# The next image's attention front inside this image's state-space scan

## The chip, the cores and the metric

The kernel runs on one core of one Trainium2 chip. The metric is the device time of one launch in microseconds (us). The kernel before took 14195.23 us, the median of three runs (14193.28 to 14201.19). The engines are called PE (TensorE), DVE (VectorE), ACT (ScalarE), POOL (GpSimd) and SP (SyncE, which only issues DMAs here).

## What is computed

Sixteen images of 192 channels and 32 x 32 = 1024 tokens (L) pass one after the other through four blocks, each added to its input X after a group norm:

1. multi-head attention: 6 heads of 32, softmax over 1024 keys, output projection;
2. a selective scan in four directions (K = 4): per direction a low-rank projection gives dt, B and C; `dt = softplus(...)`, then for each channel d and state n the recurrence `h = h * exp(dt * A) + (dt * u) * B`, and `y = sum over n of h * C`; then layer norm, gelu;
3. a depthwise 3x3 convolution of which each channel keeps its 30 largest values;
4. a chunked state-space mixer with its own convolution, gate and output projection.

```
h = h * dA + (dtt * ut)[..., None] * bt[:, :, None, :]
y = jnp.einsum('bkdn,bkn->bkd', h, ct)
```

## The kernel before, in words

`build` loads the weights and then runs a hardware loop over the 16 images (`nc.Fori`, L1666). In one pass every engine has its own in-order program, and semaphores tie them together. The blocks follow one another: `norm_*` and `attn_*` (L366 to L660), `norm_*` and `scan_*` (L756 to L1048), `conv_*`, `mix_*`. At the end of a pass the semaphores are cleared and all engines meet in a barrier (L1738 to L1741). One image ends before the next begins; only the load of the next image into XI is issued early (L1672). A scratch area of SBUF, the arena, is given anew to each block.

Attention. The projections (L457) are fp32 matmuls on the normalised image XN. Scores are needed to nearly fp32, so q and k are split into three bf16 parts (copies on ACT L567 and L571, subtractions on DVE L611 and POOL L449, 18 small DMAs per head pair by `attn_sp` L440). For every head and block of 128 queries a rough score in bf16 (L480, `rough`) gives a row maximum (DVE `reduce_max` over 128 x 1024, L617); `max_rows` (L490) turns the maxima into a row that is folded into the scores (L532, bf16). ACT takes the exponential (L597) into PT, and L548 multiplies by the values, two heads side by side in 64 columns each. `invert` (L650) and `scale` (L657) divide by the sums; L559 projects out and L642 adds to X.

The front of the scan. XN and its transpose XT are multiplied by the low-rank weights (L774, L784), softplus is done on DVE, ACT, DVE (L937, L896, L899, L942), DU = dt * u on POOL and DVE (L1028, L947). dt, dt * u, B and C are stored to DRAM (L847 to L864) and read back spread over the partitions.

The scan itself has NSTEP = 96 steps. A partition holds one (channel, state) pair, 16 channels by 8 states at a time, and a step is one such tile of 128 x 1024:

- SP (`spread`, L838, L842) brings dt and dt * u of 16 channels, 512 KB each after spreading, once for two steps, into rings of RING = 3;
- ACT (L913) writes the decay exp(dt * A) into PSUM, in two buffers, ps[1] and ps[2] by turns;
- the input product dt * u * B goes into `step[i % NBUF]`, by POOL (L1036) in one step of three, else by DVE (L991); where DVE does an even step, B is read from a copy in PSUM, made by ACT (L908), in an odd step from SBUF;
- DVE (L995) runs the recurrence along the tokens, in place;
- POOL (L1048) multiplies by C, in place;
- for each batch of 4 steps PE (L799) sums the states into ps[3], 8 fp32 matmuls of 512 columns (16 instructions in the trace), and frees four of the NBUF = 9 buffers.

DVE's program for one step is: input product if it is its own (wait for PE's batch), wait for POOL's input, wait for the decay, recurrence. POOL's is: the input product of step i + LEAD, then wait for the recurrence i, then the product with C.

```
wait_input(dve, i)
dve.wait_ge(m_da, i + 1)
nc.vector.tensor_tensor_scan(step[i % NBUF][:, o], ps[1 + i % 2][:, o], step[i % NBUF][:, o], 0.0, ALU.mult, ALU.add).then_inc(m_h, 1)
```

## Time and profile before

| | |
|---|---|
| median of three runs | 14195.23 us |
| the profiled execution | 14205.94 us |
| its span | 14204.1 us |
| busy share PE, DVE, ACT, POOL | 61%, 67%, 30%, 44% |
| mean granted TensorE clock | 0.708 of 2.4 GHz |
| image 0 begins | 39.88 us |
| image 3: attention and front of the scan | 2698 to 2982 us |
| image 3: 96 scan steps | 2982 to 3330 us |
| image 3: end of the scan, convolution, mixer | 3330 to 3584 us |

An engine's idle time costs only where nothing else sets the end; the three stages follow each other, so each is read alone. In the clock column 1.00 is 2.4 GHz and 0.50 is 1.2 GHz.

### The profile page before, as it was taken

The page shows a single profiled execution, that of the slowest core. Times are in us where ns is not written, and L with a number is a line of the kernel's source. Part 1 is how long each engine was busy: PE and PEld are TensorE (multiplying, and loading weights), DVE is VectorE, ACT ScalarE, POOL GpSimd, SP SyncE. Part 2 cuts the span into 40 slices and gives each one's busy share as a digit, 9 for nine tenths or more (in the row PEclk, how much of TensorE's full clock was granted, in tenths as well). Part 3 has the DMA queues.
Part 4 walks back from the last instruction along what each step waited for, and adds up shares of the span by engine and source line. Part 5 has one row for each costly group of instructions (what it writes and reads, how often), then busy time and mean ns, then how long its engine had stood idle before and what let it go on. Part 6 is the DMA issues. An engine that isn't in the chain of part 4 may idle for free. (4 is left out here: it accounts for less than half of the span.)

```text
span 14204.1 us, 88128 instructions
## 1 busy us (share of the span) xinstructions
PE 8617.6 (61%) x26672; PEld 2789.1 (20%) x26816; DVE 9455.2 (67%) x8214; ACT 4329.4 (30%) x4371; POOL 6226.0 (44%) x2937
## 2 busy tenths in 40 slices
PE   6475664746647466484664846648466484664846
PEld 2031221212212122121221312213122131221312
DVE  4856748567485674856758577585775857758576
ACT  2323233232332323323233232322323223232232
POOL 1815518155171551715417154271642716427164
PEclk8676776767767677676776767767676676776767
DMA  2505225052250512505135051340513405134061
GB/s 74 138 16 134 55 70 134 16 138 50 75 129 16 142 46 78 126 16 144 44 83 121 16 148 40 85 119 16 151 37 85 119 16 151 37 89 115 16 155 35
DMA packets 364229, 1164.38 MB, mean 82 GB/s; under 512 B 61487, under 2 KB 63039, under 8 KB 363599
## 3 DMA queue, kind: packets, MB, share of 16 engines
q1 hardware_dynamic: 358363, 1155.62, 32.3%
q8 instruction: 238, 3.90, 0.1%
q14 instruction: 392, 3.21, 0.1%
q10 hardware_dynamic: 3988, 1.01, 0.0%
q0 software_dynamic: 1248, 0.64, 0.0%
HBM read 959.86 MB, written 121.63 MB: 76 GB/s over the span
## 5 line engine op out<-in xcount | busy, mean ns | idle before, releaser
L799 PE MATMUL ps<-arena,sel_y 128*32 128x512 f32 x6144 | 2216.9, 888 | 3817.3 <-POOL arena L1048 3817.3
L1048 POOL TENSOR_TENSOR arena<-arena 128x1024 f32<-128x1024 f32 x1536 | 3721.7, 2449 | 29.4 <-DVE arena L995 29.4
L995 DVE TENSOR_TENSOR_SCAN arena<-ps,arena 128x1024 f32<-128x1024 f32 x1536 | 3475.8, 2284 | 66.9 <-POOL arena L1036 22.6
L913 ACT ACTIVATE ps<-arena,v_na 128x1024 f32<-128x1024 f32 x1536 | 1712.4, 1117 | 3797.8 <-DVE arena L995 3110.6
L1036 POOL TENSOR_TENSOR arena<-arena 128x1024 f32<-128x1024 f32 x512 | 1235.4, 2413 | 822.6 <-DMA arena<-scan_dtu 717.5
L799 PEld LDWEIGHTS ps<-arena,sel_y 128*32 128x32 f32 x6144 | 474.5, 151 | 5570.4 <-POOL arena L1048 3509.2
L617 DVE TENSOR_REDUCE arena<-ps 128x1 bf16<-128x1024 f32 x768 | 933.8, 1223 | 922.9 <-PE ps L480 922.4
L1028 POOL TENSOR_TENSOR arena<-arena,XN 128x1024 f32<-128x1024 f32 x32 | 75.2, 2350 | 2839.5 <-DVE arena L942 2839.5
L991 DVE TENSOR_TENSOR arena<-arena,ps 128x1024 f32<-128x1024 f32 x768 | 919.3, 1197 | 565.5 <-DMA arena<-scan_dtu 355.5
L597 ACT ACTIVATE arena<-ps 128x1024 f32<-128x1024 f32 x768 | 744.5, 1021 | 970.6 <-PE ps L532 970.6
L548 PE MATMUL ps<-arena 128*64 128x512 f32 x3072 | 773.0, 627 | 3.5 <-DVE arena L611 3.5
L532 PE MATMUL ps<-arena 65*128 65x512 bf16 (+1 forms) x2928 | 727.7, 384 | 64.1 <-ACT arena L597 29.2
L480 PE MATMUL ps<-arena 32*128 32x512 bf16 x1536 | 578.7, 468 | 105.8 <-DVE arena L617 84.8
L361 PE MATMUL ps<-g_mv,c_group 128*128 128x3 f32 (+1 forms) x512 | 136.9, 363 | 814.4 <-DVE g_mv L332 814.4
L650 DVE RECIPROCAL arena<-arena 128x256 f32<-128x256 f32 (+1 forms) x128 | 326.2, 2548 | 409.1 <-ACT arena L605 407.6
L991 DVE TENSOR_TENSOR arena<-arena 128x1024 f32<-128x1024 f32 x256 | 577.2, 2255 | 0.0
L449 POOL TENSOR_TENSOR arena<-arena 128x1024 bf16<-128x1024 f32 x48 | 101.1, 2120 | 999.5 <-ACT arena L571 999.5
L1235 PE MATMUL ps<-XN,w_x 64*128 64x512 f32 (+3 forms) x512 | 508.2, 1126 | 36.5 <-DVE XN L353 36.5
L1491 POOL TENSOR_SCALAR arena<-arena,v_mcw 128x640 f32<-128x640 f32 x144 | 164.3, 1144 | 701.3 <-ACT arena L1389 701.3
L937 DVE TENSOR_SCALAR arena<-ps,v_dtb 128x1024 f32<-128x1024 f32 x96 | 123.2, 1283 | 520.7 <-PE ps L784 520.7
L1481 DVE SCALAR_TENSOR_TENSOR arena<-arena,v_mcw 128x1024 f32<-128x1024 f32 (+1 forms) x384 | 456.9, 1190 | 13.1
L1636 POOL MEMSET arena<- 128x4624 f32 x16 | 63.2, 3951 | 909.2 <-DVE X L1121 909.2
(213 smaller groups left out, 11961.2 us busy)
## 6 DMA issues: line engine op xcount, KB each, us to landing
arena<-scan_dt SPq DMA_DIRECT2D x768, 512.0 KB, 4.7
arena<-scan_dtu SPq DMA_DIRECT2D x768, 512.0 KB, 6.0
arena<-scan_bc SPq DMA_DIRECT2D x256, 512.0 KB, 6.2
arena<-arena SPq DMA_DIRECT2D x1152, 64.0 KB, 2.0
scan_dt<-arena SPq DMA_DIRECT2D x64, 512.0 KB, 10.9
scan_dtu<-arena SPq DMA_DIRECT2D x64, 512.0 KB, 8.9
scan_dt<-arena SPq DMA_DIRECT2D x64, 256.0 KB, 12.4
scan_dtu<-arena SPq DMA_DIRECT2D x64, 256.0 KB, 12.5
```

Of the source, the lines that this page charges most:

```text
L480: mm = nc.tensor.matmul(P[:, HALF * m:HALF * m + HALF], q[:, Q * j:Q * j + Q], k[:, HALF * m:HALF * m + HALF], start=True, stop=True)
L532: mm = nc.tensor.matmul(P, k[0:n, 2 * t + e, Q * j:Q * j + Q], q[0:n, 2 * t + e, HALF * m:HALF * m + HALF], start=(n == MAIN), stop=(n == ...
L548: mm = nc.tensor.matmul(ps[2][64 * e:64 * e + 64, HALF * m:HALF * m + HALF], V[:, j - 1, 2 * t + e, :], PT[:, 2 * ((j - 1) % 2) + e, HALF ...
L597: nc.scalar.activation(PT[:, 2 * (j % 2) + e, :], ps[e][:], ACT.Exp, scale=DH ** -0.5).then_inc(a_e, 1)
L617: nc.vector.reduce_max(MX[:, i:i + 1], P[:], AX.X).then_inc(a_m, 1)
L799: mm = nc.tensor.matmul(ps[3][32 * q:32 * q + 32, HALF * h:HALF * h + HALF], sel_y[:, r, :], step[i % NBUF][:, HALF * h:HALF * h + HALF], ...
L913: nc.scalar.activation(ps[1 + i % 2][:], dtr[:, i // 2 % RING, :], ACT.Exp, scale=v_na[:, at:at + 1]).then_inc(m_da, 1)
L991: nc.vector.tensor_tensor(step[i % NBUF], dur[:, i // 2 % RING, :], states, ALU.mult).then_inc(m_buv, 1)
L995: nc.vector.tensor_tensor_scan(step[i % NBUF][:, o], ps[1 + i % 2][:, o], step[i % NBUF][:, o], 0.0, ALU.mult, ALU.add).then_inc(m_h, 1)
L1036: pool.tensor_tensor(step[i % NBUF], dur[:, i // 2 % RING, :], Bb[:, 2 * (k // 2) + f, :], ALU.mult).then_inc(m_bup, 1)
L1048: pool.tensor_tensor(step[i % NBUF], step[i % NBUF], Cb[:, 2 * (k // 2) + f, :], ALU.mult).then_inc(m_hc, 1)
L1235: mm = nc.tensor.matmul(ps[p][0:n, half(h)], w[0:m, c, lo:lo + n], XN[0:m, c, half(h)], start=(c == 0), stop=(c == 1))
```

## The change

The work is cut in two. The **front** of an image is its group norm, attention, second norm and everything up to dt, dt * u, B and C in DRAM. The rest is the 96 steps and what follows. Before the loop the front of image 0 runs alone; in the loop, pass b does the rest of image b with the front of image b + 1 woven into its 96 steps. (The front of a seventeenth image, a copy of the first, is done in the last pass.)

The weave is written out by hand. `front_pe`, `front_act`, `front_dve`, `front_pool` and `front_sp` are Python generators over HS = 192 half steps `hs`, two for each step, and each `scan_*` calls `next(front)` twice in a step:

```diff
+            for i in range(NSTEP):
+                next(front)
+                wait_input(dve, i)
+                dve.wait_ge(m_da, i + 1)
+                ...tensor_tensor_scan(step[:, i % NBUF, o], ps[2][:, o], step[:, i % NBUF, o], 0.0, ...)
+                next(front)
...
+                if i + 1 < NSTEP and not on_pool(i + 1):
+                    state_input(i + 1)
```

The plan: norm at hs 4 to 9; `project` hs 10 to 21; `values` hs 22 to 25; rough scores and their maxima from hs 16, 52 and 88, one a half step; units of scores, exponentials and head sums from hs 52 and 88 every second half step and from hs 124 every half step; output projection hs 142 and 147; second norm hs 148 to 154; low-rank projections hs 155 to 159; dt from hs 161 to 183.

```diff
+        ROUGH = [16, 52, 88]
+        UNITS = [(52, 2), (88, 2), (124, 1)]
+        DT_AT = (161, 163, 165, 172, 174, 176)
+        LN_AT = (169, 180)
+        DT_END = (170, 171, 172, 181, 182, 183)
```

The space is cut so that both fit. PSUM: ps[3] stays with the sums, ps[2] is the only decay buffer (ACT writes the decay of step i + 1 after the recurrence of step i), ps[0] and ps[1] are four half banks of 512 columns for the front. SBUF: rings of DTR = 2 and DUR = 3, NBUF = 8 step buffers, LEAD = 2. B is read from SBUF alone; its copy in PSUM goes away.

```diff
         def on_pool(i):
-            return i % 2 == 1 and i // 2 % 3 != 2
+            return i % 4 != 1
```

```diff
+            def decay(i):
+                act.wait_ge(m_dtl[i // 2 % DTR], 16 * (i // 2 // DTR + 1))
+                if i:
+                    act.wait_ge(m_h, i)
+                nc.scalar.activation(ps[2][:], dtr[:, i // 2 % DTR, :], ACT.Exp, ...).then_inc(m_da, 1)
```

Attention is rewritten for half banks. The three-way bf16 split with its copies and 54 small DMAs is gone: scores are single fp32 matmuls over 33 rows (32 of the head and one that carries the maximum), two heads at partitions 0 and 64, and the rough scores read the high halves of the same fp32 words as bf16. There are 96 rough tiles of 128 x 512 where there were 48 of 128 x 1024, and 48 units of 512 queries where there were 24 of 1024.

```diff
+                else:
+                    pe.wait_ge(a_m, 32 * t + r)
+                nc.tensor.matmul(bank(3), QR[at:at + DH, t, Q * j:Q * j + Q],
+                                 KR[at:at + DH, t, HALF * m:HALF * m + HALF], start=True, stop=True).then_inc(a_s, 1)
...
+                for e in range(2):
+                    r = slice(64 * e, 64 * e + DH + 1)
+                    nc.tensor.matmul(bank(e), KK[r, t, Q * j:Q * j + Q], QQ[r, t, HALF * m:HALF * m + HALF],
+                                     start=True, stop=True).then_inc(a_st, 1)
```

`project` pads each head to 64 columns, so it makes 12 half tiles (24 fp32 matmuls) where there were 6 (12). All six DU products are POOL's. PE's sums of batch n come in step 4n + 5, between the two half steps:

```diff
+            for i in range(NSTEP):
+                next(front)
+                if i % BATCH == 1 and i > BATCH:
+                    sums(i // BATCH - 1)
+                next(front)
```

At the start of a pass SP loads B, C, dt and dt * u of the first steps from DRAM, and the image after attention (X, YA) too, which the front of the pass before has stored (`x1_d`, `xn_d`). POOL's `conv_pool` also waits for the front's last stores (`f_out`). The convolution and the mixer are unchanged.

## Rows read from the trace of the kernel before

**Rows 1.** Page, section 1: busy us (share of the span), instructions

```profile
PE 8617.6 (61%) x26672; PEld 2789.1 (20%) x26816; DVE 9455.2 (67%) x8214; ACT 4329.4 (30%) x4371; POOL 6226.0 (44%) x2937
```

**Rows 2.** Windows, three stages: us, PE, PEld, DVE, ACT, POOL busy, clock, DMA share, GB/s

```profile
2698.00:2982.00 284.00, 214.09 (x647) 67.61 (x656) 124.18 (x123) 95.25 (x94) 19.96 (x8) 0.73 0.20 55
2982.00:3330.00 348.00, 133.60 (x368) 28.49 (x368) 309.58 (x163) 112.14 (x102) 307.56 (x128) 0.67 0.65 163
3330.00:3584.00 254.00, 189.80 (x652) 78.11 (x652) 157.65 (x227) 63.07 (x78) 60.24 (x46) 0.73 0.00 1
```

**Rows 3.** Lines by form, 2982 to 3330: busy us, mean ns, idle before, releaser

```profile
L1048 POOL TENSOR_TENSOR arena<-arena 128x1024 f32<-128x1024 f32 x96 | 232.6, 2449 | 1.9 <-DVE arena L995 1.9
L995 DVE TENSOR_TENSOR_SCAN arena<-ps,arena 128x1024 f32<-128x1024 f32 x96 | 217.2, 2284 | 3.9 <-POOL arena L1036 1.1
L913 ACT ACTIVATE ps<-arena,v_na 128x1024 f32<-128x1024 f32 x95 | 106.0, 1117 | 227.7 <-DVE arena L995 194.9 <-DMA arena<-scan_dt 32.8
L1036 POOL TENSOR_TENSOR arena<-arena 128x1024 f32<-128x1024 f32 x32 | 77.1, 2409 | 51.5 <-DMA arena<-scan_dtu 43.6 <-PE ps L799 7.8
L991 DVE TENSOR_TENSOR arena<-arena,ps 128x1024 f32<-128x1024 f32 x48 | 57.5, 1197 | 34.6 <-DMA arena<-scan_dtu 21.0 <-issue 13.6
L991 DVE TENSOR_TENSOR arena<-arena 128x1024 f32<-128x1024 f32 x16 | 36.3, 2268 | 0.0
```

**Rows 4.** Timeline, POOL and DVE in the steps: start us, us, engine, line, count

```profile
3059.22 3.35 POOL L1048 TENSOR_TENSOR arena<-arena 128x1024 f32<-128x1024 f32 x1
...
3063.82 4.47 DVE L995 TENSOR_TENSOR_SCAN arena<-ps,arena 128x1024 f32<-128x1024 f32 x2
...
3091.23 9.26 POOL L1048 TENSOR_TENSOR arena<-arena 128x1024 f32<-128x1024 f32 x4
```

**Rows 5.** Timeline, PE's sums of two whole batches (16 instructions each)

```profile
3069.53 5.65 PE L799 MATMUL ps<-arena,sel_y 128*32 128x512 f32 x16 [7.41 <-POOL arena L1048]
...
3330.11 5.09 PE L799 MATMUL ps<-arena,sel_y 128*32 128x512 f32 x16 [5.65 <-POOL arena L1048]
```

**Rows 6.** Timeline, one turn of rough score and maximum in attention

```profile
2837.26 1.94 PE L548 MATMUL ps<-arena 128*64 128x512 f32 x8
2837.37 1.23 DVE L617 TENSOR_REDUCE arena<-ps 128x1 bf16<-128x1024 f32 x1 [1.16 <-PE ps L480]
...
2839.13 0.60 PE L480 MATMUL ps<-arena 32*128 32x512 bf16 x2
...
2839.77 1.23 DVE L617 TENSOR_REDUCE arena<-ps 128x1 bf16<-128x1024 f32 x1 [1.17 <-PE ps L480]
```

**Rows 7.** Windows of attention, PE alone: us, PE busy, clock, DMA share, GB/s

```profile
2720.00:2765.00 45.00, 42.29 (x76) 0.50 0.29 71
2770.00:2825.00 55.00, 50.25 (x212) 1.00 0.12 29
```

**Rows 8.** Timeline, PE's fp32 projections, and PE in attention after a gap

```profile
2715.67 16.07 PE L457 MATMUL ps<-XN,w_qk 128*128 128x512 f32 x16 [2.38 <-DVE XN L353]
...
2830.43 3.68 PE L548 MATMUL ps<-arena 128*64 128x512 f32 x8
...
2931.07 14.02 PE L784 MATMUL ps<-arena,w_dt 12*128 12x512 f32 x16
```

**Rows 9.** Lines by form, 2698 to 2982: operations that the front keeps

```profile
L650 DVE RECIPROCAL arena<-arena 128x256 f32<-128x256 f32 x4 | 7.0, 1744 | 0.0
...
L896 ACT ACT_TABLE_LOAD x2 | 2.6, 1283 | 0.0
```

**Rows 10.** Timeline, the turn from image 2 to 3, and the start of image 0

```profile
39.88 5.21 POOL L444 MEMSET arena<- 1x6144 bf16 x1 [17.73 <-POOLq L1658]
...
2697.79 0.68 DVE L1591 TENSOR_TENSOR X<-X,ps 64x512 f32<-64x512 f32 x1 [0.32 <-PE ps L1318]
...
2708.13 2.47 DVE L320 BATCH_NORM_STATS2 g_st<-XI 128x6 f32<-128x512 f32 x4 [9.66 <-issue]
```

**Rows 11.** DMA at the start of the steps: a window (PE busy, clock, share, GB/s)

```profile
2980.00:2985.00 5.00, 0.00 (x0) 0.50 1.02 236
```

More of the change, by code:

```diff
@@ new lines, in build, with bank, unit_at, rough_at @@
+        DT_END = (170, 171, 172, 181, 182, 183)
+        def bank(i):
+            return ps[i // 2][:, HALF * (i % 2):HALF * (i % 2) + HALF]
+        def unit_at(hs):
+            for t, (at, pitch) in enumerate(UNITS):
+                if 0 <= hs - at < 16 * pitch and (hs - at) % pitch == 0:
+                    return t, (hs - at) // pitch
+            return None, 0
+        def rough_at(hs):
+            for t, at in enumerate(ROUGH):
+                if 0 <= hs - at < 36:
+                    return t, hs - at
+            return None, 0
@@ L912, in scan_act @@
+        def scan_act(act, front):
+            def decay(i):
+                _, k, j, _, _, f = STEPS[i]
+                act.wait_ge(m_dtl[i // 2 % DTR], 16 * (i // 2 // DTR + 1))
+                if i:
+                    act.wait_ge(m_h, i)
                 at = 24 * k + 2 * j + f
-                nc.scalar.activation(ps[1 + i % 2][:], dtr[:, i // 2 % RING, :], ACT.Exp,
+                nc.scalar.activation(ps[2][:], dtr[:, i // 2 % DTR, :], ACT.Exp,
                                      scale=v_na[:, at:at + 1]).then_inc(m_da, 1)
+            decay(0)
+            for i in range(NSTEP):
+                next(front)
+                if i + 1 < NSTEP:
+                    decay(i + 1)
+                next(front)
@@ L1745, in _ @@
             def _(sp):
-                sp.wait_ge(s_x, 48 * (n_batch + 1))
+                sp.sem_inc(s_out, 1)
+                for _ in front_sp(sp, 0):
+                    pass
+                front_stored(sp)
+            @block.tensor
+            def _(pe):
+                for _ in front_pe(pe):
+                    pass
+            @block.scalar
+            def _(act):
+                for _ in front_act(act):
+                    pass
+            @block.vector
+            def _(dve):
+                for _ in front_dve(dve):
+                    pass
@@ new lines, in _ @@
+            @block.gpsimd
+            def _(pool):
+                for _ in front_pool(pool):
+                    pass
+        clear()
+        with nc.Fori(0, n_batch) as b:
+            with nc.Block() as block:
+                @block.sync
+                def _(sp):
+                    scan_sp(sp, b, front_sp(sp, b + 1))
+                    front_stored(sp)
+                    sp.wait_ge(b_x, 4)
+                    for c, m in enumerate(CT):
+                        sp.dma_start(out[b, 128 * c:128 * c + m, :], X[0:m, c, :]).then_inc(s_out, 16)
+                @block.tensor
+                def _(pe):
+                    scan_pe(pe, front_pe(pe))
+                    norm_pe(pe, 2)
+                    conv_pe(pe)
+                    norm_pe(pe, 3)
+                    mix_pe(pe)
+                @block.scalar
+                def _(act):
+                    scan_act(act, front_act(act))
+                    norm_act(act, 2)
+                    conv_act(act)
+                    norm_act(act, 3)
+                    mix_act(act)
+                @block.vector
+                def _(dve):
+                    scan_dve(dve, front_dve(dve))
+                    dve.wait_ge(m_x, 4)
+                    norm_dve(dve, 2, lambda t, n: XPv[0:n, t, 1:1 + H, 1:1 + W], begun=True, room=k_z)
+                    conv_dve(dve)
+                    dve.wait_ge(k_x, 2)
+                    norm_dve(dve, 3, lambda t, n: XN[0:n, t, :])
+                    mix_dve(dve)
+                @block.gpsimd
+                def _(pool):
+                    scan_pool(pool, front_pool(pool))
+                    conv_pool(pool)
+                    mix_pool(pool)
+            clear()
@@ L1747, in _ @@
+        with nc.Block() as block:
+            @block.sync
+            def _(sp):
                 sp.wait_ge(s_out, 32 * n_batch + 1)
```

995 lines of the change are left out of this document (488 added, 507 removed).

## Prediction

> **What bounds the kernel now.** I read the shares first, and they say little: DVE is busy 67% of the span, ACT and POOL less [rows 1]. The windows say why. One image is three stages in series: 284 us of attention and front of the scan, in which PE is busy 214 and POOL 20; 348 us of scan steps, in which DVE is busy 310 and POOL 308 but PE 134; and 254 us of the rest [rows 2]. Together 886, and (14204 - 40) / 16 = 885 from the start of image 0 [rows 10]. In the first stage PE and chains through it set the pace, in the second DVE and POOL share it at 348 / 96 = 3.6 us a step, with two thirds of PE and ACT unused. The grouped lines of the steps show what fills them: recurrence 2.28, product by C 2.45, decay 1.12, input products 1.20 to 2.41 us, and 50 us in which POOL's inputs waited, mostly for a DMA [rows 3].
>
> **What goes.** The serial 284 us are taken out of each image. 9.7 of them remain, the barrier between two images [rows 10]. The front runs 17 times, once by itself. So the question is how long 96 steps take with a front in them; at 3.6 us a step they would save 4000 us, and they can't.
>
> **POOL.** It has 96 products by C, 72 input products (32 before) and 6 DU: 174 operations. Back to back one is 9.26 / 4 = 2.31 us; one that meets a DVE operation with two SBUF inputs is 3.35 [rows 4], as DVE's own is 2.27 with both inputs in SBUF where 1.20 do with one in PSUM [rows 3]. 24 input products on DVE and 6 maxima of softplus are of that kind now: 174 x 2.31 + 30 x 1.0 = 432 us, 4.3 to 4.5 a step. That is the floor, 84 over before. Moving inputs from DVE to POOL costs this; it makes room on DVE.
>
> **DVE in the rough stage.** 96 maxima of 128 x 512: a two-operand operation of that width is 0.68 [rows 10], so 0.62 in a row. Each needs a new rough score, since one half bank serves both: from the end of a maximum at 2838.60 to PE's start at 2839.13 is 0.53, and PE ends 0.04 before the next [rows 6]; with one matmul for two, 0.38, the turn is 0.95. A step has two maxima, one turn hidden under the recurrence (4.47 for two, so 2.2 [rows 4]), one not: 2.2 + 2 x 0.62 + 0.95 = 4.4. Every fourth step an input product of 2.3 fills that turn, 1.35 more. The single decay buffer (0.1 + 1.12 after the recurrence) is hidden by it. Where nothing stands there it makes 3.6 a step, under POOL's 4.3, so I cost it at nothing.
>
> **PE's sums.** A batch is 5.1 to 5.7 us when it begins at 1.2 GHz, 3.4 (16 x 0.215, from 8 in 1.94 less the last one's tail) at 2.4 [rows 5, 6]. It stands between the two half steps, ahead of a rough score for which DVE waits: it starts some 1.9 us into a step of which 4.4 are DVE's, so DVE is late by about 2.7, or 1.0 at full clock, every fourth step.
>
> **Steps, in order.** Each term is per image.
> - Steps 0 to 4, POOL's pace with the norm: 5 x 4.5 = 22.
> - Steps 5 to 12, two `project` or `values` a step. 16 instructions took 16.07 [rows 8]: 4.0 for a half tile at 1.2 GHz, near 2.0 at 2.4. With rough scores and sums a step is 10.2 or 5.4. The sums of step 5 raise the clock just before, so I take nearer the low end, 6.75: 54.
> - Steps 13 to 25, rough scores alone, PE mostly idle and so slow: 4.4 + (1.35 + 2.7) / 4 = 5.4; the last two are light: 70.
> - Steps 26 to 61, rough scores with a unit every step. Scores: 4 instructions over 33 rows, 0.85 each at 1.2 GHz by the 12-row ones [rows 8], so 3.4, half of it at full clock, and half again if two row groups run side by side; no row shows two of those. Two column groups do: L548, 8 in 1.94, is twice as fast as one after the other [rows 6]. I take side by side, 0.86 or 1.7; head sums the same. At 2.4 GHz all this fits beside DVE: 4.4 + (1.35 + 1.3) / 4 = 5.1. At 1.2 the rough score behind them comes 1.1 late and the sums 3.8: 6.9; one after the other, 8.6. Reciprocals (1.74 for 256 columns [rows 9]) and scales (0.68 like the one in [rows 10]) add 0.3. I take 5.7: 205.
> - Steps 62 to 69, two units a step. ACT's two exponentials of 0.6 and the hand-overs make 2.2 a unit, 3.5 at 1.2 GHz, plus the decay: 5.6 to 8; 6.1: 49.
> - Steps 70 to 95: 26 x 1.75 x 2.31 = 105 for POOL's products, 14 for DU, 12 for contention, 8 for two turns of ACT through table loads (1.28 [rows 9]) and three logarithms (each like a decay's 1.12), which hold up the decay behind them, 3 for slow projections before waiting copies: 142.
> - Start of a pass: barrier 9.7, then the first B, dt and dt * u from DRAM and POOL's first input, 14 more: 24. Queued there are some 17 loads of 512 KB at 240 GB/s [rows 11], 2.2 us each, so dt of step 4 lands about 12 late; two reloads of B and C later, 5: 17.
>
> Sum: 24 + 17 + 22 + 54 + 70 + 205 + 49 + 142 = 583, where 9.7 + 274 + 348 stood; with 254, **837 an image** for 885.
>
> Alone, the first front has nothing to hide in: 63 for projections at 1.2 GHz, 50 for the first rough scores, 2 x 68 with units, 45 for the last units, 66 for norm and dt, 360 in all. Setup 40 and 6 for its new loads of weights. 46 + 360 + 16 x 837 = 13800. The profiled execution was 14206 and the median 14195, which I treat as one.
>
> Nothing for: the copy of B into PSUM (7 us of ACT, hidden now), the 54 small DMAs, `f_out` (the last store is 3 steps old by then), PE's extra projection columns beyond the above. If the stores of the front come late, POOL's clearing of the border waits, and 254 grows by that.
>
> **The clock, row against rule.** PE was busy 42.3 of 45 us with projections and rough scores and the granted clock was 0.50, 1.2 GHz, throughout; then with bf16 scores over 128 rows and head sums it was 1.00 [rows 7]. Later, after a pause of PE, 8 instructions of head sums took 3.68 us where 1.94 is usual [rows 6, 8]. By the Trainium skill, "TensorE: Matmul & The Clock Gate", Part 1, sustained activity releases the throttle. By that rule every dense stretch here would run at 2.4 GHz and the sum is that of the second rival. The trace disagrees for the first 45 us, so I keep both ends. And "TensorEngine Tiling (Array Packing)", Key Properties, says that a change of tiling mode drains the array. The new PE program changes it several times a step, and no row here prices that.
>
> **Rivals.**
> 1. *Slower: PE stays at 1.2 GHz while units and rough scores share it*, and the weave turns from DVE's pace to PE's. It speaks for it that 33-row and 32-row matmuls, like L480 and L784, ran slow for tens of us [rows 7, 8]; against, that sums and head sums lift the clock [rows 5, 8]. Steps 26 to 61 at 7.2 are 259, 5 to 12 at 8.5 are 68, 62 to 69 at 7.5 are 60: 837 + 54 + 14 + 11 = 916, so 15060. It decides at 862 an image, that is at 6.4 us a step in 26 to 61.
> 2. *PE at 2.4 GHz wherever it is dense*: 5 to 12 at 5.4, 26 to 61 at 5.1, 62 to 69 at 5.6, sums of 1.0: 837 - 11 - 22 - 4 - 6 = 794, with a first front of 310: 13060.
> 3. *POOL is the bound throughout*, the front hides wholly: 24 + 17 + 432 + 254 = 727: 12040. Against it is the 4.4 + 1.0 chain, which no overlap shortens.
> 4. *It doesn't overlap*, since in-order engines wait for one another and each half step costs a whole chain. Then 274 and 348 add up as before, with 17 more for loads: 893 with the 254, 14690.
>
> **How the numbers follow.** My forecast 0.43, rival 1 0.24, rival 2 0.16, rival 3 0.08, rival 4 0.09. A measurement tells 0.2%, 28 us, from nothing. Nearly all of the forecast's spread (13400 to 14250) is faster: 0.41 + 0.16 + 0.08 = 0.65; same 0.04; slower 0.31. Range 12850 to 15050: it leaves out rival 3 and the upper half of rival 1.
>
> **What would show it.** Right: no serial attention; steps of 5 to 6 us in the rough half and about 4.4 in the last quarter, POOL over 85% busy there, DVE idle before maxima with PE as releaser, clock over 0.75 in steps 26 to 61. Wrong: steps over 6.4 there with PE over 90% busy at 1.2 GHz, PE instructions of the two heads not overlapping, DVE waiting for the decay, or long waits for DMA at a pass's start.

## The result, and the profile after

The changed kernel takes 14225.58 us, median of 20 runs (14209.24 to 14267.94), against 14199.47 us for the kernel before on the same chip: a ratio of 1.0021 [1.0014, 1.0028], the brackets being the 95% interval. The overlap works and brings nothing. The profiled execution's span is 14223.4 us, 19.3 more than before.

The page's shares show what moved. PE and POOL have more to do than in [rows 1], DVE a little less:

```profile
PE 9387.0 (66%) x27880; PEld 2830.3 (20%) x27880; DVE 9347.3 (66%) x8534; ACT 4515.9 (32%) x5590; POOL 7951.4 (56%) x3576
```

The balance comes from one instruction, the first of the mixer on POOL: count, shortest/median/longest in ns, first and last start in us (in the kernel before the same clearing, L1636, starts first at 746.4 and last at 14014.1).

```profile
L1741 POOL MEMSET arena<- x16: 3951/3951/3951, 1171.0 to 14032.4; 128x4624 f32 x16
```

A pass lasts (14032.4 - 1171.0) / 15 = 857.4 us where an image took 884.5. That gains 15 x 27.1 = 406 us. But the first mixer starts 424.6 us later, since the first image's front has nothing to hide in. 424.6 - 406.4 + 1.0 at the end is 19. So two amounts of equal size stand against each other, and each had to be forecast well.

One whole pass in windows (window, us, then busy us of PE, PEld, DVE, ACT, POOL, granted clock, DMA share, GB/s). The cuts are: last X of the pass before, recurrences of steps 0, 5, 13, 26, 62 and 70, last sums, last X. They answer to [rows 2].

```profile
3925.90:3948.80 22.90, 0.00 (x0) 0.00 (x0) 0.00 (x0) 2.40 (x2) 3.31 (x2) 0.57 0.65 166
3948.80:3995.10 46.30, 6.82 (x14) 3.19 (x16) 22.54 (x23) 8.45 (x8) 21.24 (x10) 0.50 0.71 170
3995.10:4040.10 45.00, 42.83 (x118) 14.07 (x114) 30.26 (x20) 17.74 (x24) 35.74 (x16) 0.96 0.46 111
4040.10:4104.30 64.20, 31.77 (x92) 7.46 (x94) 46.54 (x40) 15.71 (x15) 52.58 (x22) 0.61 0.43 107
4104.30:4328.50 224.20, 175.94 (x503) 39.64 (x501) 163.62 (x127) 81.15 (x113) 156.30 (x65) 0.68 0.44 105
4328.50:4376.00 47.50, 41.88 (x164) 10.11 (x160) 36.38 (x17) 25.83 (x42) 34.91 (x15) 1.00 0.31 78
4376.00:4528.60 152.60, 74.81 (x166) 19.51 (x168) 119.98 (x69) 61.10 (x60) 129.62 (x51) 0.67 0.46 131
4528.60:4783.00 254.40, 189.49 (x652) 77.37 (x652) 156.94 (x227) 63.08 (x78) 60.19 (x45) 0.73 0.00 0
```

The serial 284 us are gone and the steps take 580 to the last sums instead of 348. The stretch to understand is the fifth row, steps 26 to 61: 36 steps at 6.2 us, in which no engine is full (PE 78%, DVE 73%, POOL 70%). The grouped lines of that stretch tell what ends DVE's idle time (busy us, mean ns, then idle us before and its releasers):

```profile
L1097 DVE TENSOR_TENSOR_SCAN arena<-ps,arena 128x1024 f32<-128x1024 f32 x36 | 81.7, 2269 | 1.3 <-ACT ps L1037 1.3
L820 DVE TENSOR_REDUCE arena<-ps 128x1 bf16<-128x512 f32 x64 | 43.9, 685 | 57.8 <-PE ps L609 57.7
L833 DVE RECIPROCAL arena<-arena 128x256 f32<-128x256 f32 x8 | 13.9, 1741 | 2.4 <-ACT arena L755 2.4
L1073 DVE TENSOR_TENSOR arena<-arena 128x1024 f32<-128x1024 f32 x9 | 12.8, 1419 | 0.1
L838 DVE TENSOR_TENSOR arena<-arena 32x512 f32<-32x512 f32 x6 | 12.7, 2124 | 0.2
```

These are the recurrence (L1097), the maxima (L820), the reciprocals (L833), the input products (L1073) and the scales (L838), which divide the head sums by their denominators. 163.6 busy and 57.7 waiting for a rough score make 221 of the 224 us. DVE is either at work or waits for PE's next rough score, and hardly anything else: 4.54 + 1.60 us a step. The variants below are read by this split.

What PE did just ahead of each rough score sorts the 57.7 us (worked out from the trace's instructions): 32.9 stand behind a batch of sums (8 times, 4.1 each), 17.4 behind scores and head sums (32 times, 0.54 each), 7.4 behind another rough score (24 times).

How such a wait comes about, in the timeline (start, us, engine, line; in brackets the idle time before):

```profile
4252.47 4.08 PE L939 MATMUL ps<-arena,sel_y 128*32 128x512 f32 x16
...
4256.48 0.40 PE L609 MATMUL ps<-arena 32*128 32x512 bf16 x1
...
4256.91 0.69 DVE L820 TENSOR_REDUCE arena<-ps 128x1 bf16<-128x512 f32 x1 [3.64 <-PE ps L609]
4257.52 2.28 DVE L1097 TENSOR_TENSOR_SCAN arena<-ps,arena 128x1024 f32<-128x1024 f32 x1
```

A batch of sums takes PE 4.08 us. Behind it stands a rough score of 0.40. For this DVE waits 3.64 us, and behind DVE's maximum stands the recurrence. This is the chain that the forecast had, in its place; it is only longer.

### The profile page after: what moved, and what is told of

Read it like the earlier page. It is cut to its first block and busy times, and to the rows that moved or that the text cites. A ratio compares the mean times of both kernels' runs of the same rounds, so it can differ in the third digit from the quotient of the medians.

```text
span 14223.4 us, 93061 instructions
## 1 busy us (share of the span) xinstructions
PE 9387.0 (66%) x27880; PEld 2830.3 (20%) x27880; DVE 9347.3 (66%) x8534; ACT 4515.9 (32%) x5590; POOL 7951.4 (56%) x3576
## 5 line engine op out<-in xcount | busy, mean ns | idle before, releaser
L1150 POOL TENSOR_TENSOR arena<-arena 128x1024 f32<-128x1024 f32 x1536 | 3865.2, 2517 | 1964.4 <-DVE arena L1097 1953.4
L1097 DVE TENSOR_TENSOR_SCAN arena<-ps,arena 128x1024 f32<-128x1024 f32 x1536 | 3495.7, 2276 | 770.6 <-ACT ps L1037 688.7
L1137 POOL TENSOR_TENSOR arena<-arena 128x1024 f32<-128x1024 f32 x1152 | 2846.9, 2471 | 1369.1 <-DMA arena<-scan_dtu 1018.4
L939 PE MATMUL ps<-arena,sel_y 128*32 128x512 f32 x6144 | 1994.2, 805 | 844.4 <-POOL arena L1150 844.4
L820 DVE TENSOR_REDUCE arena<-ps 128x1 bf16<-128x512 f32 x1632 | 1116.7, 684 | 1547.2 <-PE ps L609 1546.0
L609 PE MATMUL ps<-arena 32*128 32x512 bf16 x1632 | 823.8, 505 | 1033.5 <-DVE arena L820 1033.4
L763 ACT ACTIVATE arena<-ps 128x512 f32<-128x512 f32 x1632 | 885.0, 594 | 1805.2 <-PE ps L637 1805.2
L637 PE MATMUL ps<-arena 33*128 33x512 f32 x3264 | 1208.3, 825 | 155.4 <-ACT arena L763 80.2
L649 PE MATMUL ps<-arena 128*64 128x512 f32 x3264 | 1179.5, 809 | 27.9 <-ACT arena L763 20.1
L1073 DVE TENSOR_TENSOR arena<-arena 128x1024 f32<-128x1024 f32 x384 | 707.2, 1842 | 2.0
L833 DVE RECIPROCAL arena<-arena 128x256 f32<-128x256 f32 x204 | 355.0, 1742 | 226.0 <-ACT arena L755 226.0
L1568 POOL TENSOR_TENSOR arena<-arena,c_heads 88x1536 bf16<-88x1536 bf16 x112 | 313.2, 2797 | 204.2 <-ACT arena L1522 196.2
L637 PEld LDWEIGHTS ps<-arena 33*128 33x128 f32 x3264 | 306.1, 229 | 584.6 <-ACT arena L763 285.7
```

The source lines that it names most:

```text
L609: nc.tensor.matmul(bank(3), QR[at:at + DH, t, Q * j:Q * j + Q], KR[at:at + DH, t, HALF * m:HALF * m + HALF], start=True, stop=True).then_i ...
L637: nc.tensor.matmul(bank(e), KK[r, t, Q * j:Q * j + Q], QQ[r, t, HALF * m:HALF * m + HALF], start=True, stop=True).then_inc(a_st, 1)
L649: mm = nc.tensor.matmul(bank(2)[64 * e:64 * e + 64, :], V[:, j, 2 * t + e, :], PT[:, 2 * (u % 2) + e, :], start=(j == 0), stop=(j == 7))
L763: nc.scalar.activation(PT[:, 2 * (u % 2) + e, :], bank(e), ACT.Exp, scale=DH ** -0.5).then_inc(a_e, 1)
L820: nc.vector.reduce_max(MXH[:, i // 2, i % 2:i % 2 + 1], bank(3), AX.X).then_inc(a_m, 1)
L939: mm = nc.tensor.matmul(ps[3][32 * q:32 * q + 32, HALF * h:HALF * h + HALF], sel_y[:, r, :], step[:, i % NBUF, HALF * h:HALF * h + HALF], ...
```

## The experiments

14 kernels were run, each an edit of the changed kernel where nothing else is said. "A pass" is the distance between the first recurrences of two passes in the trace, the mean unless a range is given; it is 857.4 us for the changed kernel. "A pass less" or "more" is against that. The ratios are to the kernel before. The diffs show the lines that matter; `...` marks what is left out.

**1. The front ahead of the steps instead of among them** (all five engines alike):

```diff
-                    scan_dve(dve, front_dve(dve))
+                    for _ in front_dve(dve):
+                        pass
+                    scan_dve(dve, iter(range(HS)))
```

> In each pass the front of the next image runs to its end before the first scan step; nothing else is changed. The first front alone took about 463 us in the changed kernel (60 to 503), the steps alone are bound by GpSimd at 4.3 us a step by my count, 410, with some 50 for barrier and loads and 254 for the rest. If the weave hides the shorter part as planned: 463 + 410 + 50 + 254 = 1177 a pass, 19300 in all, and the weave is worth 300 us a pass. Rival: the weave hides little, and the new front is cheap when it is alone: under 950 a pass, 15700.

Measured: 19011.18 us, ratio 1.3395 [1.3372, 1.3417], a pass of 1155 (1151 to 1158). The overlap itself is real: it is worth 298 us a pass against the same operations in series. Its steps alone take 410 us from the first to the last recurrence, in the middle 4.3 a step with POOL busy all the time, as this window of 36 such steps shows:

```profile
3380.00:3535.60 155.60, 49.71 (x144) 10.69 (x144) 100.84 (x48) 40.73 (x37) 155.60 (x65) 0.68 0.62 151
```

So the forecast's floor for POOL (4.3 to 4.5) was right. But from the last X of a pass to the next first recurrence it is 485 us; less 23 for barrier and loads, 462 are left for the front by itself, where the kernel before has 274 and the forecast took 360. And in its middle PE stays at half clock, 85% busy:

```profile
2960.00:3080.00 120.00, 101.46 (x216) 20.56 (x216) 37.32 (x49) 24.54 (x46) 0.00 (x0) 0.50 0.00 0
```

**2. Load of the next image's start later**, behind the first dt, so that the first decay comes sooner:

```diff
             spread_dt(0)
+            next(front)
             outputs(0)
...
-                next(front)
+                if i:
+                    next(front)
```

> The load of the next image's X is issued after the first dt and dt*u instead of behind some 13 loads of a pass's start. In the changed kernel VectorE waits 20 us for it in step 2, with recurrence 2 queued behind. Theory (a load behind others stops an in-order engine): step 2 starts 15 to 20 us earlier, of which the later loads of dt and C take 3 to 6 back: 11 to 16 us a pass, 180 to 260 in all, 13970 to 14050. Rival (the loads themselves are the bound at the start of a pass): the wait moves to dt and dt*u, under 4 us a pass, 14160 or more.

Measured: 14112.3 us, ratio 0.9942 [0.9925, 0.9958], 7 us a pass less. Between the two theories: the norm's wait for the image (20 us) goes, and DVE waits 12 us for ACT's part of the norm instead, which stands on ACT behind a decay whose dt is 14 us late, and 5 for decays.

**3. A batch's sums in two halves**, the first between the half steps, the second after the second:

```diff
...
-                    sums(i // BATCH - 1)
+                    sums(i // BATCH - 1, (0,))
                 next(front)
+                if i % BATCH == 1 and i > BATCH:
+                    sums(i // BATCH - 1, (1,))
```

> TensorE's sums of four steps are cut into their two half banks, one between the half steps and one after. Theory (VectorE waits for the rough score queued behind the sums, some 2.7 us every fourth step in steps 5 to 61): about 1.5 of it goes, 14 batches, 20 us a pass, 320 in all, 13900. Rival (TensorE is full in these steps, at 1.2 GHz, and its work is only moved): within 5 us a pass, 14150 to 14300; splitting may also keep the clock down, which would make it slower.

Measured: 13811.43 us, ratio 0.9735 [0.9718, 0.9751], 26 us a pass less: steps 13 to 25 took 57 instead of 64, 26 to 61 208 to 210 instead of 224. The hold of 4 us in front of a rough score is on the path. The granted clock in steps 26 to 61 rose as well, from 0.68 to 0.74, but that isn't what gained: DVE's waiting behind sums fell from 32.9 to 16.4 us, and behind scores and head sums it didn't fall (17.4 and 19.8).

**4. Scores in bf16**, to take work from PE without changing the order; leaves out the low halves of q and k:

```diff
-                    nc.tensor.matmul(bank(e), KK[r, t, Q * j:Q * j + Q], QQ[r, t, HALF * m:HALF * m + HALF],
+                    nc.tensor.matmul(bank(e), KR[r, t, Q * j:Q * j + Q], QR[r, t, HALF * m:HALF * m + HALF],
```

> The scores are made from the bf16 high halves alone, one instruction a head for two; the low halves of q and k are left out. Theory (TensorE at 1.2 GHz binds steps 26 to 61): it saves 0.43 to 0.86 us a unit, 48 units, and the rough score behind it comes earlier by as much: 20 to 35 us a pass, 350 to 550 in all. Rival (VectorE's own chain of maximum, turn, maximum and recurrence binds): under 8 us a pass, over 14100.

Measured: 14035.14 us, ratio 0.9887 [0.9871, 0.9904]. 27 us less of PE in steps 26 to 61 (149.0 for 175.9) bring 7; the first front, where PE is busy most of the time, got 80 us shorter (first recurrence at 442.2 instead of 522.4). That the steps gain so little has a second reason besides VectorE's chain. The waiting for rough scores fell by 18 us (57.7 to 39.6), but DVE's own work rose by 10.6 (163.6 to 174.2), because its nine input products took 2.84 us each instead of 1.42:

```profile
L1073 DVE TENSOR_TENSOR arena<-arena 128x1024 f32<-128x1024 f32 x9 | 25.6, 2844 | 0.1
```

They now meet more of POOL's products; what is won in one wait comes back in part as contention. The granted clock fell to 0.64, too. So this run doesn't show by itself that PE's work is nearly free in the steps.

**5. Sums in quarters**, with the later load of experiment 2:

```diff
-                if i % BATCH == 1 and i > BATCH:
-                    sums(i // BATCH - 1)
+                if i % BATCH < 2 and i >= BATCH:
+                    sums(i // BATCH - 1, (2 * (i % BATCH),))
                 next(front)
+                if i % BATCH < 2 and i >= BATCH:
+                    sums(i // BATCH - 1, (2 * (i % BATCH) + 1,))
...
```

> Based on the two changes measured before it (load of the next image later: 7 us a pass less; sums of a batch in two halves: 24 a pass less), with each batch's 16 matmuls now in quarters of four, one at the end of each half step from step 4n+4 to 4n+5. Theory (what costs is the longest stretch for which PE keeps a rough score waiting, so that halving it again gives about half as much again): 24 x 0.4 = 10 us a pass more, 13811 - 113 - 160 = about 13540. Rival (the first quarter now stands half a step after the product it needs, PE waits there for POOL with a rough score behind it, or the halves already hid under the recurrence): no further gain, 13700 or more.

Measured: 14044.89 us, ratio 0.9889 [0.9872, 0.9905], on the rival's side, and far above its 13700. The sums took PE 2996.6 us in the run instead of 2065.7 with halves and the later load (experiment 9). A quarter held two matmuls into the same 32 output columns, where a half holds both output tiles side by side.

**6. The rough score ahead of scores and head sums** in each half step:

```diff
+                if t is not None and 0 < r < 32:
+                    rough(t, r)
                 t, k = unit_at(hs)
                 if t is not None:
                     scores(t, k)
...
-                if t is not None and r < 32:
+                if t is not None and r == 0:
                     rough(t, r)
```

> In each half step PE's rough score goes ahead of the scores and the head sums instead of behind them. Theory (DVE's 57.7 us of idle time before maxima in 225 us of steps 26 to 61 come from rough scores that stand behind 2.2 to 4 us of scores and head sums): some 0.8 us a step less over 36 steps and a little in the two groups before, 30 us a pass, about 13750. Rival (PE itself is what is full in these steps, or the scores now wait for the maximum and with them the exponentials, so only the order changes): within 5 us a pass, 14150 to 14300.

Measured: 14388.38 us, ratio 1.014 [1.0123, 1.0157]: both theories missed, 11 us slower in steps 26 to 61. DVE's waiting for rough scores rose from 57.7 to 68.2 us. ACT's for scores went from 86.2 to 135.9. That fits a rough score which waits for its maximum and now keeps the scores behind it waiting, as the rival said.

**7. The scales left out** (the division by the denominators; the twelve 32 x 512 products become a clearing of the same cells):

```diff
-                            nc.vector.tensor_tensor(OA[...], OC[r:r + 32, :], RD[r + 32:r + 64, :], ALU.mult)
+                            nc.vector.memset(OA[...], 0.5)
```

> Leaves out the division of the head sums by their denominators: the twelve products of 32 x 512 of a front, 2.04 us each beside GpSimd and 0.68 without, are replaced by clearing the same cells. Theory (small VectorE operations with two SBUF inputs wait for a whole GpSimd operation, and this waiting is on the path): 12 x 1.8 = 20 us a pass less, 13900 to 13950. Rival (VectorE waits for PE right after them in any case, so their waiting is taken out of a later wait): 5 us a pass or less, 14150 or more.

Measured: 14059.42 us, ratio 0.9904 [0.9887, 0.992], 10.4 us a pass over the whole run, between the two. In steps 26 to 61 DVE's busy time fell by 6.8 us and the steps by 3.8: a good half of what DVE is spared counts, the rest becomes waiting for PE (57.7 to 60.2).

**8. The overlap alone, with the input products split as before** (64 by VectorE, 32 by GpSimd):

```diff
-            return i % 4 != 1
+            return i % 2 == 1 and i // 2 % 3 != 2
...
+            state_input(0)
```

> The overlap alone: VectorE makes 64 of the 96 input products and GpSimd 32, as before the change. Theory (VectorE's chain of maximum, recurrence, maximum, input product sets the step, and GpSimd has room): 40 more products on VectorE, each 1.84 to 2.3 us of which one turn of the rough score is filled, some 1.1 net each: 44 us a pass slower, about 14900. Rival (GpSimd is the bound, it drops from 174 operations to 134): up to 40 us a pass faster in the steps, 13600. If both share it, near 14225.

Measured: 14504.11 us, ratio 1.0221 [1.0204, 1.0238], 17 us a pass more. A window of steps 26 to 61:

```profile
4188.20:4420.80 232.60, 173.31 (x504) 39.38 (x503) 209.20 (x143) 81.31 (x113) 123.08 (x49) 0.69 0.39 100
```

DVE has 46 us more to do than in the changed kernel and the steps take 8 more; the rest fills waits for PE (57.7 to 19.4).

**9. The two edits that gained, together** (experiments 2 and 3).

> Both edits that gained alone, together: the sums of a batch in two halves (24 us a pass less) and the load of the next image's start behind the first dt (7 us a pass less). If they act in different steps, as their traces say (the one in steps 13 to 61, the other in steps 0 to 4), they add up: 14225 - 414 - 113 = about 13700. Rival (a step won in one place is waited for in another): 13770 or more.

Measured: 13690.92 us, ratio 0.9643 [0.963, 0.9656], a pass of 823.8. They add up: 414 and 113 less would be 13698. This kernel computes the same as the reference and is faster than the kernel before and the changed one.

**10. Quarters with both output tiles** (experiment 5 with `2 * h + i % 2` instead of `2 * h + i % BATCH // 2`):

> Quarters again, at the same places as before, but each holds one product of either output tile instead of two of the same tile. Theory (the quarters were slow because two matmuls into the same 32 columns run one after the other, where those into different columns run side by side, so PE's sums took 2997 us instead of 2063): sums near 2063 again, and the time at or under that of halves with the later load, 13550 to 13700. Rival (the quarters are slow because each starts at the low clock, or because the first of them waits for GpSimd's product with a rough score behind it): still 13900 to 14050.

Measured: 13870.34 us, ratio 0.9796 [0.9745, 0.9846]: the theory on the columns holds for most of PE's sums (2305.4 us after 2996.6, with 2063 foretold), not for the time, which lies between theory and rival. Its passes are not alike. Steps 26 to 61 of two passes of the same execution:

```profile
7366.30:7563.30 197.00, 159.47 (x489) 31.85 (x485) 163.47 (x127) 79.18 (x110) 158.30 (x66) 0.77 0.49 121
11467.00:11697.40 230.40, 194.73 (x484) 35.51 (x482) 164.87 (x130) 78.86 (x109) 162.87 (x67) 0.60 0.43 105
```

Same instructions, nearly the same DVE and POOL time; the granted clock is 0.77 in one and 0.60 in the other, PE takes 35 us more and the steps take 33 more. Nearly all of that is DVE's waiting for rough scores behind scores and head sums, 44.4 us instead of 16.6; behind the sums it is 11.0 and 6.4. This is the price of the clock in these steps. What lowered it in the one pass isn't shown.

**11. Two more matmuls over 128 rows for each unit**, results not used:

```diff
                 for e in range(2):
+                    nc.tensor.matmul(bank(e), c_identb[:], QR[:, t, 0:HALF], start=True, stop=True)
+                for e in range(2):
                     r = slice(64 * e, 64 * e + DH + 1)
```

> The changed kernel with two more bf16 matmuls of 128 rows and 512 columns ahead of each unit's scores, into the banks that the scores overwrite; their result is not used. Theory (TensorE's clock is what costs: it is granted 0.68 of full speed in steps 26 to 61, and what lifts it is work over all 128 rows): granted clock 0.9 or more in those steps and in the first front, PE's instructions there a third shorter, 15 to 30 us a pass less although 0.45 us a unit is added, about 13850, and the first front 100 us shorter. Rival (the clock doesn't follow the added rows, or VectorE's chain sets these steps anyway): 0.4 to 0.8 us a unit more, 48 units, 20 to 40 us a pass more, 14600 to 14900.

Measured: 14362.71 us, ratio 1.0111 [1.0096, 1.0126], first recurrence 19 us later. In steps 26 to 61 the clock was 0.76 instead of 0.68 and the time 225.2 us instead of 224.2. It didn't reach 0.9, and in the first front the scores kept their 2.08 us for most of the time. PE was busy 7 us more, with the added work in it. DVE waited 8 us less for rough scores (57.7 to 49.7) and worked 8 us more, with input products of 2.45 us instead of 1.42. So the higher clock did shorten the waits, and as in experiment 4 contention took the gain back. Steps 62 to 69 took 5 us more.

**12. GpSimd makes all input products of steps 13 to 69**, on top of experiment 9 (`i % 4 != 1 or 13 <= i < 70`):

> The two-part version in which GpSimd makes all input products of steps 13 to 69, 14 of which VectorE made. Theory (VectorE's chain sets these steps at 5.8 us and GpSimd, with two products of 2.31, has room): 14 x 1.1 = 15 us a pass less than the two-part version, about 13450. Rival (the input product fills a wait for PE's rough score, and more GpSimd work makes more of VectorE's small operations wait): within 5 us a pass of the two-part version, 13650 to 13800.

Measured: 13815.09 us, ratio 0.9735 [0.972, 0.9749]. Just outside the rival, and 124 us slower than experiment 9. DVE had 10 us less to do in steps 26 to 61, and these took 210 to 218 us in different passes, 213 on average, against 209. At a clock of 0.74 they took 210, as in experiment 9 at the same clock; the longer ones had 0.69 to 0.73. Steps 13 to 25 took 5 us more (62). So in steps 26 to 61 what it costs goes with the lower clock. Of the three splits that were run, every fourth input product on VectorE is the fastest; nothing between them was tried.

**13. Half of the rough scores and maxima left out**, those that stand ahead of a step's recurrence; a row's maximum is then that over half of its scores:

```diff
+                elif r % 2:
+                    return
                 else:
-                    pe.wait_ge(a_m, 32 * t + r)
+                    pe.wait_ge(a_m, 16 * t + r // 2)
...
```

> Leaves out every second half of the rough scores: 48 of the 96 matmuls and maxima of a front, the ones that stand ahead of the recurrence of a step; a row's maximum is then that over half of its scores. Theory (a step of the middle is VectorE's own work and what it waits for the second rough score of the step; no engine is full): without that turn, 0.68 of maximum and 1.6 of waiting a step, steps 26 to 61 take 165 to 180 us instead of 224, and 13 to 25 about 55 instead of 64: 50 to 65 us a pass less, 13200 to 13450. Rival (what sets these steps is PE's work at the low clock, 176 us of 224, and the turns only follow it): 16 us less of PE, 205 or more in steps 26 to 61, 13850 or more.

Measured: 13089.73 us, ratio 0.922 [0.9206, 0.9234], a pass of 790 (784 to 797), and a first front 62 us shorter. That is more than the theory's 13200. The same 36 steps:

```profile
3760.10:3933.90 173.80, 138.05 (x470) 32.49 (x468) 148.61 (x95) 79.15 (x112) 159.66 (x67) 0.79 0.57 135
```

50 us less, with POOL now 92% busy. DVE waits 9.2 us for rough scores where it waited 57.7, works 15 less, and waits 14 more for decays and POOL's inputs. A bound by PE's work alone was to leave 205 or more. PE's 38 us less go beyond the 16 that were taken out, as the clock rose to 0.79. That can explain only the waits that are left: the rough scores behind scores and head sums, 17.4 us before and 9.2 now. The other 40 us of waiting stood ahead of rough scores that are no longer made.

**14. The last image without a front**, on top of experiment 9: the loop runs 15 times, and a copy of the pass with empty fronts follows.

```diff
-        with nc.Fori(0, n_batch) as b:
+        with nc.Fori(0, n_batch - 1) as b:
...
+                scan_sp(sp, n_batch - 1, iter(range(HS)))
```

> The two-part version with the last image outside of the loop and without the seventeenth front, which nothing uses. Theory (a front costs its pass what it costs elsewhere: 543 us of steps with it, about 410 without as in the run with the front ahead of the steps): 130 us less once, 13560. Rival (the code of a second copy of the pass has to be fetched, or the last pass runs into the end of the stores): 60 us less or nothing, 13630 to 13690.

Measured: 13558.68 us, ratio 0.9552 [0.9539, 0.9565], as forecast. The last pass's 96 steps take 415 us instead of 542. This is the fastest kernel with the reference's computation:

```profile
12877.50:13292.30 414.80, 130.32 (x368) 28.12 (x368) 269.07 (x123) 106.20 (x95) 403.49 (x166) 0.65 0.58 139
```

## Why the forecast was wrong, step by step

The forecast was 13800 and faster; the kernel is 0.2% slower. 13800 + 93 for the start + 16 x 20.4 for the passes = 14219, so two terms hold nearly the whole miss of 426. That the time still lies in the stated range is no merit of the sum: the gain it forecast is gone whole.

**The first front: 360, measured 453.** The first recurrence starts at 522.4; less 22.9 for the barrier and first loads and 46 of setup, 453 are left, nine of them before the first projection. Projections and values took 68 (63 forecast), rough scores before the units 36 (50), the 32 units with rough scores among them 194 (2 x 68), the last units 64 (45), the rest 82 (66). The step that failed is "2 x 68 with units". In the timeline a unit with its two rough scores looks like this, over and over:

```profile
301.09 0.60 PE L609 MATMUL ps<-arena 32*128 32x512 bf16 x1 [0.79 <-DVE arena L820]
301.63 2.08 PE L637 MATMUL ps<-arena 33*128 33x512 f32 x4
303.64 1.97 PE L649 MATMUL ps<-arena 128*64 128x512 f32 x4
305.54 0.60 PE L609 MATMUL ps<-arena 32*128 32x512 bf16 x1
306.93 0.60 PE L609 MATMUL ps<-arena 32*128 32x512 bf16 x1 [0.79 <-DVE arena L820]
307.47 2.08 PE L637 MATMUL ps<-arena 33*128 33x512 f32 x4
```

5.84 us a unit, five of them PE at 1.2 GHz. I had taken 4.2, halfway to full clock. There are no sums of the scan here, and experiment 1 shows the clock at 0.50 in just this work. Experiment 4 shows that PE is on the path: cheaper scores made this front 80 us shorter.

**The pass: 837, measured 857.4.** Start 63 (24, 17 and 22), measured 69.2. Steps 5 to 12: 54, measured 45.0, at a clock of 0.96. Steps 13 to 25: 70, measured 64.2. Steps 26 to 61: 205, measured 224.2. Steps 62 to 69: 49, measured 47.5. Steps 70 on: 142, measured 152.6. The rest: 254, measured 254.4. Steps 5 to 25 came out 15 us under the forecast, which by luck hid part of the miss. The step that failed is "I take 5.7: 205"; it is 6.2. Three parts of it:
- The *mechanism* was right: DVE's own time plus the turn with PE's rough score. Experiment 13 shows it, by taking the second turn away: 48.5 of the 57.7 us of waiting went. The forecast's 5.7 is about 4.3 of DVE's own work (2.2, 1.24 for maxima, 0.57 for a quarter of an input product, 0.3) and 1.4 of waiting; measured are 4.54 and 1.60. So the miss of 0.5 a step is about half own work and half waiting.
- *PE's sums* were priced at 5.1 to 5.7 us cold and 3.4 warm, with a delay of 2.7 or 1.0 for DVE. They took 4.08 in the row above and DVE waited 3.64; the mean of the eight in steps 26 to 61 is 4.1, over the 2.7 of the cold price. That is 32.9 us or 0.91 a step where the forecast had 0.25 to 0.68, and the largest part of the waiting. The units, 2.08 + 1.97 us cold where the forecast had 3.4, make 17.4 more. Experiment 3 shows what the block of sums costs: cut in two it gives back 14 to 16 us of steps 26 to 61.
- *Contention was priced for 30 DVE operations, as a cost of POOL.* DVE pays too, on operations that the forecast had at their quiet price, "scales (0.68 ...)". The groups of the whole run:

```profile
L838 DVE TENSOR_TENSOR arena<-arena 32x512 f32<-32x512 f32 x204 | 417.0, 2044 | 6.4
L862 DVE TENSOR_SCALAR arena<-arena 128x1024 f32<-128x1024 f32 x102 | 166.1, 1628 | 217.1 <-ACT arena L782 217.1
L372 DVE TENSOR_SCALAR XN<-XI,g_t 128x512 f32<-128x512 f32 x102 | 141.7, 1417 | 1.2
L355 DVE TENSOR_TENSOR g_t<-g_t 128x2 f32<-128x2 f32 x66 | 78.4, 1188 | 2.2
```

In the first front, with POOL idle, the same operations take 0.68, 1.05, 0.54 and 0.17 us. The scales' excess is 12 x 1.4 = 17 us of DVE's time a pass; six of them stand in steps 26 to 61, 8.6 us or 0.24 a step. The own work there has other misses as well: reciprocals and scales were put at 0.3 a step together, took 0.74, and would have been 0.50 with quiet scales, while an input product was put at 2.3 us and took 1.42, 0.36 a step for 0.57. Experiment 7 prices the scales on the path: 10 us a pass for some 19 of DVE's time taken out. The Trainium skill, "SBUF — State Buffer", Who interferes with whom, says that a VectorE instruction with two SBUF inputs contends with a GpSimd instruction that reads SBUF, that one in a two-port mode, which `tensor_scalar` can enter, contends too, and that in that mode the engine which issues first keeps the shared ports for its whole instruction. By that rule every one of these lines was open to waiting, and the traces agree: the 32 x 512 product takes 0.68 us alone and 2.04 in the whole run beside POOL. The reciprocals (one input) kept their 1.74, as in [rows 9].

**Start of a pass: 17 for stalls.** The timeline of DVE there:

```profile
3952.43 2.29 DVE L1097 TENSOR_TENSOR_SCAN arena<-ps,arena 128x1024 f32<-128x1024 f32 x1 [0.20 <-ACT ps L1037]
3974.70 2.46 DVE L336 BATCH_NORM_STATS2 g_st<-XI 128x6 f32<-128x512 f32 x4 [19.98 <-DMA XI<-in_x]
...
3977.58 2.29 DVE L1097 TENSOR_TENSOR_SCAN arena<-ps,arena 128x1024 f32<-128x1024 f32 x1
```

The amount was nearly right and its owner wrong. I had put it on dt of step 4; what DVE waits for, 20 us a pass, is the next image, loaded behind everything else, with recurrence 2 queued behind the norm that needs it. Experiment 2 shows that the loads as a whole stay the limit: only 7 of the 20 come back.

**Steps 70 on: 142, measured 152.6.** POOL is busy 129.6 us there, and 131 were priced (105, 14 and 12). It is idle for 23 where the forecast had 11, so the term that was too small is POOL's waiting. DVE in turn waits 8.7 us for decays and 4.5 for input products. Of the norm's small operations the forecast made nothing:

```profile
4404.53 2.00 DVE L347 TENSOR_TENSOR g_mv<-g_mv 128x2 f32<-128x2 f32 x1
...
4408.95 2.27 DVE L355 TENSOR_TENSOR g_t<-g_t 128x2 f32<-128x2 f32 x1
...
4411.33 2.20 DVE L358 TENSOR_TENSOR g_t<-g_t 128x2 f32<-128x2 f32 x1
...
4415.82 5.16 DVE L372 TENSOR_SCALAR XN<-XI,g_t 128x512 f32<-128x512 f32 x2
```

11.6 us for what takes some 1.6 alone, with recurrences behind them; three of the four rows are operations on two columns. I read this from the trace; no run took it away.

**The rivals.** The first, PE at 1.2 GHz, put steps 26 to 61 at 7.2 us a step and the pass at 916. The clock there is 0.68, a mixture, and experiment 10 shows what the rival is worth: 33 us a pass between 0.77 and 0.60. So the passes came out between the forecast and this rival, at 6.2 us a step, and the rival was right for the first front, to which I hadn't applied it. The second rival, full clock wherever PE is dense, fails in the windows (0.50 at 85% busy, experiment 1); it holds in steps 5 to 12 and 62 to 69. "TensorE: Matmul & The Clock Gate", Part 1, of the Trainium skill says that sustained activity releases the throttle. The front in series disagrees: its granted clock is 0.50 for some 380 us on end, with PE busy throughout 60 of them (2837 to 2897). The third rival's 12040 had POOL as the bound; it is the bound in the steps only when nothing is among them (experiments 1 and 14). The fourth, no overlap, is refuted by experiment 1. Its sum had a slip besides: 274, 348, 17 and 254 leave out the 9.7 of the barrier, so it stood for 903 a pass and 14850.

**The signs.** Of those named for "right", the serial attention is gone, POOL is 85% busy at the end, and DVE does wait ahead of maxima for PE. Steps 26 to 61 took 6.2 us and those at the end 5.9, not 5 to 6 and 4.4, and the clock was 0.68, not over 0.75. Of those named for "wrong", the long wait for DMA at a pass's start is there (20 us).

**Which part of the change did what.** Moving inputs from VectorE to GpSimd is worth 17 us a pass (experiment 8). Without it the overlap would gain 10 a pass and lose 425 at the start. The rewritten attention is the price of the overlap: the front by itself takes 462 where 274 stood. No run separates its parts (half tiles, single fp32 scores, padded heads, and a clock of 0.50 where the kernel before had 1.00 in part); bf16 scores give 80 us of it back (experiment 4).

What stays open: what makes passes warm or cold in experiments 10 and 12, and how much of steps 70 on is contention.

## What to carry to other kernels

Overlapping a stage of one pass with the pass before it (software pipelining) has two prices that the steady state doesn't show: the stage that fills it, run alone and at its own clock, and the useless one at the end. Here 15 times 27 us won in the passes were eaten by 425 us of filling; cost the filling stage by itself, and take the last pass out of the loop (132 us). Where engines meet in many short turns, ask of every long block (here sums of 4 us) what short instruction stands behind it and who waits for that. Cutting that block in two was worth 26 us a pass, more than the 17 of moving the input products. But keep in each piece what runs side by side (experiments 5 and 10). And a wait that is shortened can come back as contention elsewhere (experiments 4 and 11): read own work and waiting apart.

## What the runs showed of the hardware

- Two heads' fp32 matmuls over 33 rows run largely side by side, and the head sums follow them without a gap. In the steps, just after a batch of sums:

```profile
4256.81 1.13 PE L637 MATMUL ps<-arena 33*128 33x512 f32 x4
...
4257.86 1.08 PE L649 MATMUL ps<-arena 128*64 128x512 f32 x4
```

  1.13 us for four instructions of 512 columns at full clock and 2.08 at half; the forecast's 0.86 and 1.7 were too low by 0.27 and 0.38, and one after the other it would be 1.7 and 3.4. The head sums begin 0.08 us before the modelled end of the scores. The forecast left open what "TensorEngine Tiling (Array Packing)", Key Properties, of the Trainium skill says, that a change of mode drains the array. No such time shows between these two groups; whether some of the 0.27 us is it, the runs don't tell.
- The granted clock shown ahead of the first change in a trace says nothing: the first front is shown at 1.00 until 424 us, but its instructions take 2.08 and 1.97 us, to the hundredth what they take in the front of experiment 1, where the record says 0.50.
- The granted clock falls into a few patterns. In experiment 10 steps 26 to 61 take 197.0, 198.3, 201.8, 219.5 to 219.7, 226.0, 227.3 or 230.3 us in the 16 passes of one execution, 201.8 in six of them, with clocks from 0.78 down to 0.62. In the changed kernel all 16 passes take 224.2 to 224.3. A change of order can move a kernel from one pattern to another, so a difference of up to 33 us a pass between variants need not be the edit's own; compare the clocks, and the waits one by one.
- A VectorE operation on two columns can take 2.0 to 2.3 us beside GpSimd's product where it takes 0.17 by itself. A product of 128 x 1024 with both inputs in SBUF takes 1.20 us where it meets none (changed kernel, 3951.02), 1.42, 2.45 and 2.84 on average in steps 26 to 61 of the changed kernel and of experiments 11 and 4.
